# A decoder layer on one core: softmax weights left unnormalised, each head's output scaled in PSUM by reciprocals that go through DRAM

## The reference, cut to what matters

```python
scores = jnp.einsum('blhd,bmhd->bhlm', q, k) * scale      # 4 batches, 16 heads, 512 x 512, causal
attn = jax.nn.softmax(scores, axis=-1)
out = jnp.einsum('bhlm,bmhd->blhd', attn, v)
x = x + out.reshape(B, L, H * DV) @ w_o
```

## Time and profile before

| | us |
|---|---|
| median of 3 runs | 1166.24 (1164.35 to 1167.4) |
| the profiled execution | 1167.31 |
| its span, first to last instruction | 1165.5 |
| PE busy in the span | 957.6 (82%) |
| DVE busy | 963.2 (83%) |
| ACT busy | 643.6 (55%) |

### The profile page before, as it was taken

One profiled execution on the slowest core, in us unless ns is written; L12 is line 12 of the kernel. 1 busy time (PEld: TensorE's weight loads), 2 busy tenths in 40 slices (PEclk: granted clock), 3 DMA queues, 4 the chain that ended last, 5 costly groups with the idle time before them and its releaser, 6 DMA issues.

```text
span 1165.5 us, 17748 instructions
## 1 busy us (share of the span) xinstructions
PE 957.6 (82%) x5622; PEld 546.8 (47%) x5640; DVE 963.2 (83%) x2902; ACT 643.6 (55%) x1437; POOL 249.7 (21%) x268
## 2 busy tenths in 40 slices
PE   0446567889999999999999999999978655559997
PEld 0324333554554555555555555555535444435553
DVE  5767748999888988998998988988968898857885
ACT  1446546666555656656656656666513675753442
POOL 1036522122112112212212212112100113221211
PEclk9769789999999999999999999999989888769999
DMA  9300004534433446443436433335364530002434
GB/s 346 145 1 1 10 8 85 93 76 80 94 67 78 81 78 154 84 74 78 88 77 151 77 70 68 68 63 136 71 212 109 146 103 6 1 0 37 80 85 91
DMA packets 247661, 98.19 MB, mean 84 GB/s; under 512 B 221832, under 2 KB 233096, under 8 KB 247056
## 3 DMA queue, kind: packets, MB, share of 16 engines
q1 hardware_dynamic: 247568, 97.06, 36.6%
HBM read 36.06 MB, written 7.34 MB: 37 GB/s over the span
## 4 chain that ended last, share of the span: by engine, by line
DVE 48%; PE 34%; ACT 7%; issue 6%; DMA 3%; POOL 2%; SPq 0%; DVEq 0%; ACTq 0%; POOLq 0%
PE bank L1964 8%; PE bank L1912 5%; DVE bank L1541 4%; DVE arena L1558 4%; PE bank L1858 4%; PE bank L1949 4%; DVE arena L1565 4%; DVE arena L797 3%; PE bank L1891 3%; DVE arena L715 2%; DVE arena L717 2%; DMA arena<-arena 2%; DVE arena L681 2%; DVE arena L1572 2%; DVE arena L1525 2%
## 5 line engine op out<-in xcount | busy, mean ns | idle before, releaser
L1241 ACT ACTIVATE arena<-bank,arena 128x128 f32<-128x128 f32 (+3 forms) x256 | 134.3, 525 | 108.2 <-DVE arena L1541 106.7
L1964 PE MATMUL bank<-arena 128*128 128x512 f16 x768 | 180.3, 383 | 1.9 <-DVE arena L1591 1.9
L1565 DVE SCALAR_TENSOR_TENSOR arena<-arena 128x128 f16<-128x128 f32 (+3 forms) x256 | 144.3, 564 | 9.1
L1541 DVE CUSTOM_DVE_ANT_0 bank<-bank,maskb,scal 128x128 f32<-128x128 f32 (+3 forms) x256 | 141.4, 552 | 12.1 <-PE bank L1937 11.6
L1949 PE MATMUL bank<-arena 128*128 128x512 f16 (+3 forms) x768 | 119.7, 308 | 33.6 <-DVE arena L1572 24.6
L1912 PE MATMUL bank<-arena 128*128 128x512 f16 x576 | 137.2, 384 | 0.0
L1949 PEld LDWEIGHTS bank<-arena 128*128 128x128 f16 x768 | 72.8, 100 | 92.9 <-issue 46.4
L1558 DVE TENSOR_SCALAR arena<-arena 128x128 f16<-128x128 f32 (+3 forms) x256 | 109.0, 426 | 7.3 <-DVE arena L1550 0.3
L1964 PEld LDWEIGHTS bank<-arena 128*128 128x128 f16 x768 | 74.0, 99 | 82.9 <-issue 6.0
L1087 POOL TENSOR_TENSOR arena<-arena 128x512 f32<-128x512 f32 x32 | 45.3, 1415 | 308.7 <-ACT arena L1261 308.5
L1261 ACT ACTIVATE arena<-bank 32x512 f32<-32x512 f32 x128 | 75.2, 588 | 30.9 <-PE bank L1891 29.6
(11 more groups left out here) (200 smaller groups left out, 1892.8 us busy)
## 6 DMA issues: line engine op xcount, KB each, us to landing
arena<-arena SPq DMA_TRANSPOSE x308, 2.7
arena<-in_L_attn_w_qb SPq DMA_DIRECT2D x1, 4608.0 KB, 21.0
arena<-in_x SPq DMA_DIRECT2D x4, 1024.0 KB, 6.0
arena<-in_L_attn_w_o SPq DMA_DIRECT2D x1, 4096.0 KB, 31.4
arena<-in_fside_BxS2xS SPq DMA_DIRECT2D x4, 1024.0 KB, 8.2
arena<-in_L_ffn_w SPq DMA_DIRECT2D x8, 512.0 KB, 7.9
out<-arena SPq DMA_DIRECT2D x16, 256.0 KB, 2.4
arena<-in_x SPq DMA_DIRECT2D x12, 256.0 KB, 2.9
```

Of the source, the lines that this page charges most:

```text
L1241: act.activation(pf(k), banks[S_BANKS[G % 3]][:, 0:n].rearrange("p (t c) -> p t c", c=P), ACT.Exp, bias=NB[:, k:k + 1], scale=-1.0, accum_ ...
L1541: dve.tensor_tensor_reduce(s, s, maskb[:, L - n:L], nsc_exp, 3e38, ALU.add, ALU.min, NB[:, (g & 3):(g & 3) + 1]).then_inc(s_max, 1)
L1565: dve.scalar_tensor_tensor(out=ph_part(k, 1), in0=pf(k), scalar=R4[:, k:k + 1], in1=ph_part(k, 0), op0=ALU.mult, op1=ALU.subtract).then_in ...
L1964: last = pe.matmul(banks[Y_BANK][:, :], ot(gp, a, k, (q & 3) * P, P), wo(b, gp * GH + k), start=(k == 0 and n == 0), stop=(k == GH - 1 and ...
```

## The change

`row_scale` runs once for a head and takes four reciprocals at once. The exponentials are multiplied by the constant 4096 alone. SP stores the 512 reciprocals of a head to DRAM (`store_sums`) and loads them back, spread over all 128 partitions (`spread_sums`), into `RB`. A new DVE instruction, `out_norm`, multiplies the head's output in PSUM by them, in place; it reads `RB` with a step of four fp32 numbers. `out_hi` now waits for `out_norm`. `values` alternates between two banks; the second is the former `P_BANK`, so `prep_mm` of later batches shares the bank of the even heads. Slots move on ACT, DVE, PE, SP and POOL. The load of a token tile (`load_xt`) now goes into `XN`, and waits until that is read.

```diff
+            def store_sums(Hd):
+                sp.wait_ge(s_rc, Hd + 1)
+                sp.dma_start(rc_dram[Hd].rearrange("(q t) -> q t", t=TB),
+                             RC[:, (Hd & 1) * TB:(Hd & 1) * TB + TB]).then_inc(rc_out[Hd & 1], 16)
+            def spread_sums(Hd):
+                sp.wait_ge(rc_out[Hd & 1], 16 * (Hd >> 1) + 16)
+                if Hd >= 2:
+                    sp.wait_ge(o_nrm, Hd - 1)
+                sp.dma_start(RB[:, (Hd & 1) * L:(Hd & 1) * L + L],
+                             rc_dram[Hd].partition_broadcast(P)).then_inc(rc_in[Hd & 1], 16)
...
@@ sync, in the loop over i and g
+                    if g in (3, 7):
+                        store_sums(2 * i + (g >> 2))
+                    if g == 5:
+                        spread_sums(2 * i)
+                    if g == 1 and i > 0:
+                        spread_sums(2 * i - 1)
                     turn_probs(i, g)
...
             def out_hi(Hd):
-                act.wait_ge(pv_mm, Hd + 1)
-                act.activation(ot(gpar, 0, slot, 0, L), banks[O_BANK][:, :], ACT.Copy).then_inc(o_hi, 1)
+                act.wait_ge(o_nrm, Hd + 1)
+                act.activation(ot(gpar, 0, slot, 0, L), banks[O_BANKS[Hd & 1]][:, :], ACT.Copy).then_inc(o_hi, 1)
...
-            def row_scale(G, g):
-                k = g & 3
-                dve.wait_ge(s_exp, G + 1)
-                dve.reciprocal(RC[:, k:k + 1], SUM[:, k:k + 1]).then_inc(s_rc, 1)
-                dve.wait_ge(s_rc, G + 1)
-                dve.tensor_scalar(R4[:, k:k + 1], RC[:, k:k + 1], PSCALE, None, ALU.mult).then_inc(s_r4, 1)
+            def row_scale(Hd):
+                h = Hd & 1
+                dve.wait_ge(s_exp, 4 * Hd + 4)
+                if Hd >= 2:
+                    dve.wait_ge(rc_out[h], 16 * (Hd >> 1))
+                dve.reciprocal(RC[:, h * TB:h * TB + TB], SUM[:, h * TB:h * TB + TB]).then_inc(s_rc, 1)
...
-                dve.tensor_scalar(ph_part(k, 0), pf(k), R4[:, k:k + 1], None,
+                dve.tensor_scalar(ph_part(k, 0), pf(k), PSCALE, None,
...
+            def out_norm(Hd):
+                h = Hd & 1
+                dve.wait_ge(pv_mm, Hd + 1)
+                dve.wait_ge(rc_in[h], 16 * (Hd >> 1) + 16)
+                o = banks[O_BANKS[h]].rearrange("p (t q) -> p t q", t=TB)
+                dve.tensor_tensor(o, o, rb(h), ALU.mult).then_inc(o_nrm, 1)
...
@@ tensor, values and pair
-                if not (i == 0 and h == 0):
-                    pe.wait_ge(o_lo, Hd)
+                if Hd >= 2:
+                    pe.wait_ge(o_lo, Hd - 1)
...
-                    if (j, g) == (0, 2):
+                    if (j, g) == (0, 3):
                         if prep is not None:
                             if started(i - 5):
                                 pe.wait_ge(y_added, i - 4)
+                            if not first:
+                                pe.wait_ge(o_lo, 2 * i - 1)
                             prep_mm(prep[0])
```

More of the change, by code:

```diff
@@ L133, in decoder_layer @@
         small = take(40)
-        NB, SUM, RC, R4 = (small[:, 20 + 4 * k:24 + 4 * k] for k in range(4))
+        NB, SUM, RC = small[:, 20:24], small[:, 24:32], small[:, 32:40]
         rstd = small[:, 10:11]
@@ L1599, in pair @@
                         if not first:
-                            row_scale(G - 1, 7)
+                            row_scale(2 * i - 1)
                             probs_hi(i - 1, 7)
                             probs_lo(G - 1, 7)
+                            out_norm(2 * i - 2)
+                    if (j, g) == (0, 1):
+                        probs_hi(i, 0)
+                        probs_lo(G + 0, 0)
+                        if not first:
                             out_lo(2 * i - 2)
-                    if (j, g) == (0, 1):
-                        row_scale(G, 0)
-                        probs_hi(i, 0)
-                        probs_lo(G, 0)
                         if started(i - 5):
@@ L1611, in pair @@
                     if (j, g) == (0, 2):
-                        row_scale(G + 1, 1)
                         probs_hi(i, 1)
                         probs_lo(G + 1, 1)
+                    if (j, g) == (0, 3):
+                        probs_hi(i, 2)
+                        probs_lo(G + 2, 2)
                         if prep is not None:
@@ L1649, in pair @@
                     if (j, g) == (1, 0):
-                        if not first:
-                            row_scale(G - 1, 7)
-                            probs_hi(i - 1, 7)
-                            probs_lo(G - 1, 7)
-                            out_lo(2 * i - 2)
+                        row_scale(2 * i - 1)
+                        probs_hi(i - 1, 7)
+                        probs_lo(G - 1, 7)
+                        out_norm(2 * i - 2)
                     if (j, g) == (1, 1):
-                        row_scale(G, 0)
                         probs_hi(i, 0)
-                        probs_lo(G, 0)
+                        probs_lo(G + 0, 0)
+                        out_lo(2 * i - 2)
                     if (j, g) == (1, 2):
-                        row_scale(G + 1, 1)
                         qn_lo_(2 * i + 1, 1)
@@ L1683, in pair @@
                             prep_xn(ahead)
-                        if not first:
-                            out_lo(2 * i - 1)
                     if (j, g) == (1, 6):
-                        row_scale(G + 5, 5)
                         if not last:
@@ L1691, in pair @@
                         probs_lo(G + 5, 5)
+                        out_norm(2 * i - 1)
                     if (j, g) == (1, 7):
-                        row_scale(G + 6, 6)
                         if ahead is not None:
@@ L1852, in prep_mm @@
                     pe.wait_ge(xn_in, 16 * (n - TB) + 16)
-                for lo, wid, bank, done in ((0, QL, P_BANK, qa_mm), (QL, KVL + DR, Y_BANK, kv_mm)):
+                for lo, wid, bank, done in ((0, QL, qa_bank(n), qa_mm), (QL, KVL + DR, banks[Y_BANK], kv_mm)):
                     k = 0
```

105 lines of the change are left out of this document (54 added, 51 removed).

## The result

The changed kernel took 1211.36 us (median of 4 runs), beside 1165.49 us for the kernel before. One of the four runs, of 1997.88 us, was disturbed and is left out of the comparison, in which the other three (1209.07 to 1212.87, median 1209.86) give 1.0385 times as long, 95% interval 1.0357 to 1.0414. The forecast was 1181 us, 1154 to 1197. The direction was right; the loss is 45 us by the ratio, where 15 were forecast. The profiled execution took 1209.86 us, its span is 1208.0, 42.5 longer than before.

What follows compares the result with a forecast made beforehand. DVE bounds at most the first four pairs, PE the later ones. Terms 3.0 - 4.4 + 3.7 + 8.8 + 3.4 make plus 14.5 on the profiled 1167.3 us, 1181.8, or 1181 as median; range 1154 to 1197.

Steps and rivals of the forecast that it cites:

- The wait of `values` goes.: With two banks `values` no longer waits for `out_lo`; 24.6 us can go at most.
- Even pair with `prep`: `project` waits 2.5 us in pairs 4 to 20, plus 3.0; in the others scores wait 0.55 us, minus 4.4.
- T+6.7: Even pair with `prep`: `rotate` and the keys' rotary sum end 6.7 us after the end of `prep_mm`.
- T+7.5, hidden under that: POOL's 1.42 and 1.29 us behind the swap end 7.5 us after `prep_mm`, hidden under `row_max` and `exps`.
- `out_norm`: DVE's new multiply of a head's output takes 0.68 us, bounds 0.68 and 1.56.
- Clock: Slow matmuls after PE's waits at `project`: three times 1.7 us, less one: plus 3.4, bounds minus 1.7 to plus 10.2.
- Slots 0 and 1, and pairs without `prep`: `prep_mm` waits 0.7 us for `add_y` in 10 pairs, plus 3.7; longer waits in pairs 24 to 30, plus 8.8.
- First four pairs: Pairs before `project` starts: no change, 0, bounds minus 10 and plus 4.
- DVE's relief: Reciprocals and multiplies per block go, fewer instructions come back; DVE's busy time down by some 45 us.
- DMA and the end: Store and load of reciprocals, 5.8 us, hidden by some 11 us of slots; 0.7 us more at the end is free.
- D: Rival: `out_norm` is slow, 1.56 us, because of its step; 13 us in `prep` pairs, 1196 us; chance 0.12.
- B: Rival: DVE's relief reaches PE, the waits of `values` go and nothing takes their place; 1140 us; chance 0.24.

Runs made afterwards that it cites:

- run 6: Kernel before with one thing alone changed, two output banks; no deferred division, no slot moved: 1154.54 us, ratio 0.9910.
- Run 2: Changed kernel with the keys' rotary sum of `prep` ahead of `rotate`, so that it runs before POOL does: 1173.99 us, ratio 1.0076.
- run 1: Changed kernel without any division: no `out_norm`, no store or load of reciprocals, exponentials multiplied by 8 in place of 4096: 1192.81 us, ratio 1.0242.
- run 9: Changed kernel's arithmetic and two banks in the slots of the kernel before, with `out_hi` of the odd head ahead of `qn_hi_`: 1159.81 us, ratio 0.9950.
- run 4: Changed kernel with reciprocals stored in pieces of 4 bytes, so that `out_norm` reads them without a step: 1466.02 us, ratio 1.2588.
- run 7: Changed kernel's slots and banks, with the division block by block as before; no `out_norm`, no DMA of reciprocals: 1216.53 us, ratio 1.0430.
- run 3: Changed kernel with the odd head's output (`out_norm`, `out_hi`, `out_lo`) one slot earlier: 1167.07 us, ratio 1.0023.
- runs 5: Changed kernel with the odd head's output one slot earlier and the rotary sum ahead of `rotate`, both at once: 1170.47 us, ratio 1.0047.
- run 10: Changed kernel with `prep` alone back in the slots of the kernel before, the output's chain left as changed: 1210.02 us, ratio 1.0366.

## Why the prediction was right in direction and wrong in size

*The wait of `values` goes.* Right, and worth 11 us alone (run 6).

*Even pair with `prep`.* The mechanism was right: `out_hi` behind `rope_hi` (the earlier trace rows against the lines above), `project` waiting for `out_lo` in every fourth pair and the scores for `qn_lo_` in the others. The size was not, and this is the step that failed. The stepping had `rotate` and the rotary sum end at T+6.7. The `row_max` behind them started at T+8.2, since the sum, 1.3 us by forecast, took 2.67 us beside POOL. The wait was 3.97 us where 2.5 was forecast, and 1.98 where 0.55 was: 5 x 1.47 + 4 x 1.43 is 13 us of the missing 20 between pairs 4 and 22. The prediction moved the sum next to POOL's instructions ("T+7.5, hidden under that") and asked only who waits for POOL, not what POOL does to DVE. The 1.56 us that it took for the second half of `prep_split` and for the upper bound of `out_norm` was already such a meeting. Run 2, which takes the sum out of POOL's way, shows the cost.

*`out_norm`.* Taken as 0.68, it was 1.08. The bounds held. In the `prep` pairs the wait is shorter by 0.27 us without any `out_norm` at all (3.97 against 3.70 of run 1), so the longer time costs no more than that there.

*Clock.* This term was mis-sized too. Three stretches of 1.7 us were forecast for all of the walk, less one. There were five of 1.7 to 2.5 us behind the waits of 3.97 us, 11.7 us in all, and one of 1.6 in pair 28: more than the upper bound of the term, and the other 7 us of the missing 20. Waits and slow stretches make 45.5 us between pairs 4 and 22, against 21.0 before; the difference of 24.5 is nearly all of the 25.7 measured.

*Slots 0 and 1, and pairs without `prep`.* Right: `prep_mm` waits 0.67 us (0.7 forecast), the scores 1.27 (1.4), `project` 2.45 (2.15), the next scores 0.46 (0.15). From pair 22 on it is 12.4 us, 8.8 forecast; 1.3 of it is the longer wait of pair 22 and 1.6 the slow stretch of pair 28.

*First four pairs.* Wrong: 0 forecast, +4.0 measured like for like, at the bound. The first scores of pairs 1 and 3 waited 3.60 and 4.57 us for `qn_lo_`, on the same chain, 5.1 us more than at the same places before (2.09 and 1.02); the other waits and slow stretches there came out a little shorter in sum. In run 9, where `out_hi` is ahead of `rope_hi`, these two are 2.0 and 1.9.

*DVE's relief.* Forecast -45 us busy, measured -21.1 (963.2 to 942.1): 256 reciprocals and multiplies took 80 us, and 11 + 69 came back for `row_scale` and `out_norm`, so the exchange alone was level. `probs_hi` and `probs_lo`, counted as 0, gave 30 us (the constant operand, and a block that met POOL before and no longer does), and `prep` beside POOL took 12. (These are sums of durations, 18 us in all; in the busy time neighbours that overlap count once.)

*DMA and the end.* Right: no wait for the reciprocals that matters, and nothing lost behind the last `values`.

Of the rivals, D had its mechanism in run 4. In waits it had a fifth of its price, some 2.4 us of 13; the 9.2 us of slow matmuls that went in run 1 can't be put down to `out_norm` or the DMAs, since run 7 has neither and its matmuls are slow in all five places, after 4.02 us. B is what the same arithmetic does in other slots, though at 1148 us. A reading of run 3 alone ("the output's place makes the loss") and of run 2 alone ("POOL makes it") each seems complete. They are one chain, cut at two places, as runs 5 and 10 show. What stays open is why the same PE slows in five of five places after 3.97 us of waiting and in one of five after 3.70. The length of the wait alone does not tell: in run 10 the matmuls were slow in five of five after 3.0 to 3.2 us, in run 2 in two of five after 2.17. No run varied the wait and nothing else.

## What to carry to other kernels

Ask what each moved instruction now runs beside, not only what it waits behind: an instruction of 64 elements can take the whole of another engine's 1.26 us. A copy that frees a buffer belongs ahead of long work on its engine, not behind it. And before a bundle of edits is given up, time its parts: here the two banks were a gain of some 10 us, the arithmetic was level, and the order of the slots lost some 60.

## What the runs showed of the hardware

A DVE instruction that starts beside a POOL one can be held to its end. `TENSOR_SCALAR` of 128x64 took 254 ns alone and 1193 in the mean of 12 beside POOL; of 128x2, 222 and 632. The first ended 0.06 us after POOL's in pair 12. A `CAST` of 128x512 that started 0.11 us after POOL's L1129 took 1.33 us; in another run (9) it took 0.42. A `TENSOR_TENSOR` of 128x512 with both operands in SBUF (the second half of `prep_split`) took 1.64 us beside POOL and 0.69 without. `rotate`, which has one operand in PSUM, took its 0.69 us beside POOL's L1118 too. The Trainium skill (SBUF — State Buffer, section "Who interferes with whom") says that the two engines share a pair of ports by an exclusive lock, held for a whole instruction by whichever came first, and names `tensor_scalar` and `cast` among those that can take it. The trace agrees.

A second operand read with a step of 16 bytes made a 128x512 multiply in PSUM 1.55 times as long (medians of 1074 and 692 ns). The Trainium skill (SBUF — State Buffer, section "Door 1: The DMA port swizzle"), by whose rule on lines of 16 bytes the prediction named rival D, is borne out in direction; the size is this case's.

`probs_lo` and `probs_hi` with a constant in place of a per-partition number: 128x128 blocks 292 and 286 ns, against 351 and 346 before. Run 7, with the changed slots and the per-partition number, has 351 for `probs_lo` again, and its longer blocks differ from the changed kernel's by 59 to 61 ns too.

A 2 KB store in 512 pieces of 4 bytes landed after 10.2 us, in 128 pieces of 16 bytes after 1.7, and for the turned probabilities behind it in SP's queue PE waited up to 11.4 us.
